# Queries of all tiles projected ahead of the attention loop, together with keys and values

## The reference, cut to what matters

```python
x = x + _L0_cond_ref(x, ...)   # paged attention
x = x + _L1_cond_ref(x, ...)   # 64x64 mix of the tokens, one of 8 weights per batch
x = x + _L2_cond_ref(x, ...)   # x @ W_base.T + low-rank adapter, 1 of 4 per batch
x = x + _L3_cond_ref(x, ...)   # x @ W.T + low-rank adapter, 1 of 8 per batch
```

```python
q = _rope(_rms(q, q_norm_scale), pos)     # rms over the 64 of a head
k = _rope(_rms(k, k_norm_scale), pos)
k_blocks = k_blocks.at[blk, :, off, :].set(k.transpose(0, 2, 1, 3))
v_blocks = v_blocks.at[blk, :, off, :].set(v.transpose(0, 2, 1, 3))
```

## Time and profile before

| what | us |
|---|---|
| median of three runs | 433.83 (431.53 to 435.05) |
| the profiled execution | 432.4 |
| its span, first to last instruction | 430.3 |
| TensorE busy | 414.3 |
| VectorE, ScalarE, GpSimd busy | 308.1, 225.3, 263.7 |

### The profile page before, as it was taken

The page is one execution under the profiler, slowest core; times in us unless marked ns, Lnnn a source line. Parts: engine busy times, 40 slices in busy tenths (PEclk is TensorE's granted clock), DMA queues, the critical chain, the costliest instruction groups (busy, mean ns, idle before and its releaser), DMA issues.

```text
span 430.3 us, 9867 instructions
## 1 busy us (share of the span) xinstructions
PE 414.3 (96%) x2890; PEld 306.0 (71%) x2890; DVE 308.1 (72%) x901; ACT 225.3 (52%) x590; POOL 263.7 (61%) x242
## 2 busy tenths in 40 slices
PE   5999999999899999999999999999999999999987
PEld 1434456846477788887887888778888788788776
DVE  3989797568497777777777767777777777776642
ACT  1232211367356575655756565657566575656641
POOL 3388536655878776767667686767676766734000
PEclk9999999999999999999999999999999999999999
DMA  7187767893655646465564646645565655533211
GB/s 219 44 283 258 259 207 225 249 344 99 199 134 139 195 126 187 121 163 162 137 187 134 189 124 188 145 141 158 145 162 136 171 150 133 145 110 97 56 52 50
DMA packets 76267, 69.08 MB, mean 161 GB/s; under 512 B 50517, under 2 KB 52693, under 8 KB 76215
## 3 DMA queue, kind: packets, MB, share of 16 engines
q1 hardware_dynamic: 57248, 42.03, 33.6%
q0 software_dynamic: 15456, 22.08, 19.3%
q10 hardware_dynamic: 3510, 4.35, 2.8%
HBM read 78.39 MB, written 11.93 MB: 210 GB/s over the span
## 4 chain that ended last, share of the span: by engine, by line
PE 74%; DVE 9%; issue 5%; DMA 4%; POOL 4%; ACT 3%; ACTq 0%; DVEq 0%; POOLq 0%; SPq 0%
PE banks L1131 30%; PE banks L1284 10%; PE banks L1264 9%; PE banks L1144 8%; PE banks L1121 6%; PE banks L1299 4%; POOL windows L529 3%; PE banks L1322 3%; DVE x L902 2%; DMA windows<-kvrows_dram,idx_all 2%; ACT x L677 2%; PE banks L1312 2%; DMA kvb<-kvl_dram 1%; PE banks L1125 1%; DVE prob L989 1%
## 5 line engine op out<-in xcount | busy, mean ns | idle before, releaser
L529 POOL DMA_INDIRECT windows<-newkv,idx_all x78 | 79.3, 1017 | 29.5 <-issue 21.6
L529 POOL DMA_INDIRECT windows<-kvrows_dram,idx_all x78 | 78.6, 1007 | 25.2 <-issue 24.6
L649 ACT ACTIVATE pt_s<-banks 112x384 f32<-112x384 f32 x128 | 56.2, 500 | 64.4 <-PE banks L1121 64.4
L643 ACT ACTIVATE prob<-prob,negmax 128x336 f32<-128x336 f32 x128 | 72.1, 564 | 24.4 <-DVE negmax L989 24.4
L499 POOL TENSOR_TENSOR rstd<-ms,half 128x8 f32<-128x8 f32 x24 | 45.5, 1896 | 54.4 <-DVE ms L922 34.1
L989 DVE CUSTOM_DVE_ANT_0 prob<-banks,mask 128x336 f32<-128x336 f32 x128 | 57.5, 504 | 11.8 <-PE banks L1264 11.4
L1144 PE MATMUL banks<-wkv_s,xt_s 128*128 128x512 f32 x128 | 59.0, 617 | 5.6 <-DMA xt_s<-xt_dram 5.6
L1144 PEld LDWEIGHTS banks<-wkv_s,xt_s 128*128 128x128 f32 x128 | 24.4, 195 | 37.4 <-issue 26.8
L999 DVE TENSOR_SCALAR prob<-prob,rinv 128x336 f32<-128x336 f32 x128 | 45.9, 401 | 2.3
L1264 PE MATMUL banks<-kt_s,qt_s 64*128 64x336 f32 x256 | 44.8, 468 | 0.0
L1131 PE MATMUL banks<-wf_hi,x 128*128 128x512 f32 x120 | 41.7, 408 | 3.0 <-DVE x L902 1.9
(11 more groups left out here) (213 smaller groups left out, 827.6 us busy)
## 6 DMA issues: line engine op xcount, KB each, us to landing
usel<-utab SPq DMA_DIRECT2D x64, 128.0 KB
xt_s<-xt_dram SPq DMA_DIRECT2D x31, 256.0 KB, 4.6
newkv<-kvo SPq DMA_DIRECT2D x16, 256.0 KB, 3.6
stage<-xtok_dram SPq DMA_DIRECT2D x16, 256.0 KB, 13.0
tsel<-ttab SPq DMA_DIRECT2D x64, 64.0 KB
out_dram<-xo ACTq DMA_DIRECT2D x15, 256.0 KB, 6.0
windows<-kvrows_dram,idx_all POOLq DMA_INDIRECT x78
windows<-newkv,idx_all POOLq DMA_INDIRECT x78
```

What stands on the lines that cost most here:

```text
L529: P.indirect_dma_start(kv_s[i][:, c, :], None, newkv if new else kvrows, bass.IndirectOffsetOnAxis(ap=idx_all[:, new * CH + c, b:b + 1], a ...
L643: A.activation(pr, pr, ACT.Exp, bias=negmax[:, g:g + 1], scale=-1.0, accum_out=psum_p[b % 2][:, g:g + 1]).then_inc(S["exp_done"], 1)
L649: A.activation(pt_s[g][:], tb[g % 2][0:KP, 0:CH * 128].rearrange("p (c q) -> p c q", c=CH), ACT.Copy).then_inc(S["pt_ev"], 1)
```

## The change

- The tokens are loaded once. In the front stage ACT rounds each tile (`x_high`), DVE takes the rest (`x_low`), into two alternating buffers `x_s`. From tile 3 on keys and values use these split words with split `wkv` weights, twelve matmuls per tile; tiles 0 to 2 remain plain fp32.
- Each tile's queries follow its keys (tiles 0 to 2 in a row after three key tiles). ACT copies them to `qraw` (128 x 16 x 512 in SBUF) and squares them, DVE sums (`query_sums`) and takes the mean for two tiles, POOL makes the roots of two tiles in one 128x16 power (`root_queries`).
- In the loop `queries`, the reload and split of the tokens, the square, the sums and the root are gone. `query_first` and `query_last` (the rotation) are now in odd k, two tiles ahead, between the mask copy and `ranks` on DVE, and read `qraw`.
- The key banks are two pairs in turn instead of three; queries use banks 4 and 5. Weights of queries and of keys share the places of `wo_s` and `wf_s`. POOL gathers old rows of windows 1 to 3 ahead of the new rows, with the last roots between.

The core of the diff:

```diff
+            x_high(0)
+            for c in range(C):
+                act.wait_ge(l_wkv[c], 16)
+                A.activation(wkv_s[0][:, c], wkv_raw[:, c], ACT.Copy).then_inc(S["wkv_hi"], 1)
...
+            x_high(2)
+            query_ev(0)
+            act.wait_ge(S["tab_ready"], 1)
+            A.activation(nsinx, rest, ACT.Sin, scale=-1.0)
...
+            x_high(3)
...
+            for i in range(2, PAIRS):
+                x_high(2 * i + 1)
+                query_ev(2 * i - 1)
...
+                if 2 * i + 2 < TILES:
+                    x_high(2 * i + 2)
+                query_ev(2 * i)
+                key_pair(i)
...
+            def root_queries(i):
+                pool.wait_ge(S["q_ms"], i + 1)
+                two = [x[:, 2 * i:2 * i + 2, :].rearrange("p t h -> p (t h)") for x in (q_rstd, q_ss)]
+                P.tensor_tensor(two[0], two[1], half[:], ALU.pow).then_inc(S["q_rstd"], 1)
...
+            key_pair(0)
+            query_means(0)
+            for i in range(1, PAIRS):
+                if 2 * i + 3 < TILES:
+                    x_low(2 * i + 3)
+                query_sums(2 * i)
+                if i == 7:
+                    query_first(0)
+                    query_last(0)
+                key_pair(i)
+                if 2 * i + 4 < TILES:
+                    x_low(2 * i + 4)
+                query_sums(2 * i + 1)
+                query_means(i)
+                if i == 1:
+                    index_first()
...
+                if i == 4:
+                    index_rows()
...
             low(t3tab[:, :, :, 0].rearrange("p e c r -> p c e r"), t3tab[:, :, :, 1].rearrange("p e c r -> p c e r"),
                 ob[:].rearrange("p (c e r) -> p c e r", c=C, e=NE3), "t3_hi", 1, "t3_ev")
-            xq_low(1)
+            query_first(1)
+            query_last(1)
...
-                    if t + 2 < TILES:
-                        xq_low(t + 2)
                     if n < NB:
                         mask_at(n)
+                    if t + 2 < TILES:
+                        query_first(t + 2)
+                        query_last(t + 2)
                     if t >= 1:
                         ranks(t - 1)
...
+            def key_tile(n):
+                pe.wait_ge(S["x_lo"], n + 1)
+                if n == PLAIN:
+                    pe.wait_ge(S["wkv_lo"], C)
+                dense3(key_banks(n), lambda p, c: x_s[n % 2][p][:, c, :], lambda p, c: wkv_s[p][:, c, :]).then_inc(S["ka_mm"], 1)
...
+            for n in range(PLAIN):
+                key_tile_plain(n)
+            for t in range(PLAIN):
+                queries(t)
+            for n in range(PLAIN, TILES):
                 key_tile(n)
+                queries(n)
+                if n == 3:
+                    index_blocks()
+                if n == 7:
+                    index_lose()
+                if n == 9:
+                    index_win()
...
                 if k % 2 == 0:
-                    if t + 1 < TILES:
-                        queries(t + 1)
                     keys_t(n)
```

More of the change, by code:

```diff
@@ L163, in build @@
         wcode = sb("wcode", [NB, NW * BLOCK], f16)
-        wt_tok = sb("wt_tok", [NB, NW * BLOCK])
-        wt_ge = sb("wt_ge", [NB, NW * BLOCK])
         idx_all = sb("idx_all", [KP, 2 * CH, NB], i32)
[L167 to L174, removed]
+        half = sb("half", [128, 16])
+        t1, t2 = sb("t1", [128, 8, 64]), sb("t2", [128, 8, 64])
+        wt_tok, wt_ge = (t[0:NB].rearrange("p h d -> p (h d)")[:, 0:NW * BLOCK] for t in (t1, t2))
+        kvi = t1[:].rearrange("p h d -> p (h d)")[:, 512 - NB:512].bitcast(i32)
+        ss, ms, rstd = sb("ss", [128, 8]), sb("ms", [128, 8]), sb("rstd", [128, 8])
+        q_ss, q_rstd = sb("q_sums", [128, TILES, 8]), sb("q_roots", [128, TILES, 8])
         [qrot_w] = words([("qrot_w", [128, 512])])
@@ L259, in build @@
         l_wkv = [sem(f"l_wkv{i}") for i in range(C)]
+        l_wq = [sem(f"l_wq{i}") for i in range(C)]
         l_stage = [sem(f"l_stage{i}") for i in range(STAGES)]
@@ L269, in build @@
         block = ctx.enter_context(nc.Block())
-        splits = [(w[0][:, c], w[1][:, c], src[:, c]) for w, src in ((wq_s, wq), (wo_s, wo)) for c in range(C)]
+        splits = [(wo_s[0][:, c], wo_s[1][:, c], wo[:, c]) for c in range(C)]
+        PLAIN = 3
         PAIRS = TILES // 2
@@ L356, in spread_rows @@
                                  rows.rearrange("p k (c s b) -> p k c s b", c=CH, s=SP_)[:, :, :, s, :]).then_inc(S["idx_ready"], 16)
-            load_keys_x(0)
+            load_x(4)
+            load_x(5)
+            load_x(6)
+            load_x(7)
+            store_pair(0)
+            load_x(8)
+            sp.dma_start(b2_s, b2t).then_inc(S["l_low"], 16)
+            sp.dma_start(a2_s, a2t).then_inc(S["l_low"], 16)
+            load_x(9)
+            store_pair(1)
+            load_rows(wpt_s, wpt, "l_wpt")
+            load_x(10)
+            load_x(11)
+            store_pair(2)
+            sp.wait_ge(S["wkv_lo"], C)
+            load_rows(wt_s, wt, "l_wt")
+            load_x(12)
+            load_x(13)
+            store_pair(3)
+            sp.wait_ge(S["wq_lo"], C)
+            load_rows(wbn_s, wbn, "l_wbn")
+            load_x(14)
+            load_x(15)
+            store_pair(4)
+            spread_rows()
+            sp.dma_start(a3_s[:], a3t).then_inc(S["l_low3"], 16)
+            sp.dma_start(b3_s[:], b3t).then_inc(S["l_low3"], 16)
+            sp.wait_ge(S["qtab_ready"], 1)
+            load_rows(w3_s, w3, "l_w3")
+            store_pair(5)
             load_split(0)
@@ L533, in gather @@
                     ).then_inc(kv_in[i], 16)
-            root("k", 7, 0)
             pool.wait_ge(S["idx_ready"], 16 * SP_)
-            root("q", 1, 1)
             gather(0, 0)
-            root("k", 8, 0)
+            root_keys(6)
+            root_queries(5)
             gather(1, 0)
+            root_queries(6)
+            gather(2, 0)
+            root_keys(7)
+            gather(3, 0)
+            root_queries(7)
             pool.wait_ge(S["row0_stored"], 16)
@@ L602, in evac @@
                 A.activation(dst, src, ACT.Copy).then_inc(S[done], 1)
+            x_high(0)
+            for c in range(C):
+                act.wait_ge(l_wkv[c], 16)
+                A.activation(wkv_s[0][:, c], wkv_raw[:, c], ACT.Copy).then_inc(S["wkv_hi"], 1)
+            x_high(1)
+            for c in range(C):
+                act.wait_ge(l_wq[c], 16)
+                A.activation(wq_s[0][:, c], wq_raw[:, c], ACT.Copy).then_inc(S["wq_hi"], 1)
             key_pair(0)
@@ L950, in _, with split_low @@
+            def split_low(k):
+                dve.wait_ge(S["split_lo"], k)
+                low(splits[k][0], splits[k][1], stage[k % STAGES][:], "split_hi", k + 1, "split_lo")
+            split_low(0)
             low(t2tab[:, :, :, 0].rearrange("p e c r -> p c e r"), t2tab[:, :, :, 1].rearrange("p e c r -> p c e r"),
```

389 lines of the change are left out of this document (159 added, 230 removed).

## The result

The changed kernel takes 455.53 us (median of four runs, 450.81 to 456.01), the kernel before 433.25 (431.53 to 435.05) in the same comparison. The ratio is 1.049, with a 95% interval of 1.042 to 1.056: slower. Forecast were 448.7 us and a range of 439 to 457. The profiled execution is the shortest one, 450.81 us, with a span of 449.0.

What follows compares the result with a forecast made beforehand. TensorE, busy 96%, looked like the bound, but a loop tile without queries waits for attention's low part and saves only 1.77 us. Terms 41.4 - 10.5 - 0.8 + 0.7 + 5.0 - 1.0 - 18.5 = +16.3 on 432.4 gave 448.7 us, range 439 to 457.

Steps and rivals of the forecast that it cites:

- Queries moved to the front: Front stage: fifteen query groups of 2.76 us come to stand before the first folding matmul, +41.4 us.
- Keys in three products: Front stage: thirteen key tiles go from plain fp32 at 3.57 us to split words at 2.76, -10.5 us.
- Waits of the front: Front stage: tile 4's wait for tokens goes, -0.8 us; a new wait before key tile 3, +0.7 (bounds 0 and 2).
- The front ends at 101.8: End of front: first folding matmul moves from 71.04 to 101.8 us by the query, key and wait terms.
- Gathers: First window's keys: POOL's queue of roots and gathers delivers late, so TensorE waits about 5.0 us (0.8 with cheap roots).
- Start of the loop: Loop start: first projection comes 1.0 us earlier relative to the keys, -1.0 us (at most -5.5).
- Loop: Main loop: thirteen tiles lose a query group, gaining 1.42 us each, -18.5 us.
- The rotation's delay: Loop, odd half: rotation between mask and ranks' split on VectorE makes the split 0.35 us late per tile (bounds 0 and 0.7).
- TensorE stays the bound: Rival, whole kernel: every matmul spared in the loop counts, -11.3 us, giving 421.1 us; chance 0.07.
- The losses hide: Rival: roots cost as before, rotation fits before the ranks, loop start gains 5.5; +2.4 us, 434.8 us; chance 0.07.
- The front is bound by VectorE: Rival, front: VectorE's work exceeds a pair's 11.0 us, TensorE waits up to 2 us four times; 457 us; chance 0.12.

Runs made afterwards that it cites:

- experiment 7: Changed kernel with key tiles 3 to 15 as one fp32 product of rounded tokens and weights instead of three split-word products: 460.47 us.
- experiment 5: Changed kernel, order untouched, with 35 extra unread matmuls of 128x512 in TensorE's waits at the start of the loop: 449.37 us.
- experiment 1: Changed kernel with the rotation of a tile's queries moved from the odd half to the even half, between mask and first residual: 445.69 us.
- experiment 6: Extra unread matmuls in each even half but the first: four in the changed kernel, 451.23 us; twelve, plus 8 at loop start, in the both edits kernel, 465.44 us.
- both edits: Changed kernel with rotation in the even half and GpSimd's queue reordered: 444.51 us; with 20 extra unread matmuls at loop start, 441.63 us.

## Why the prediction was right, and by how much it missed

The class was right, and so were the waits and prices that it named, with sizes off by up to 2.7 us. That the median lies in the range is in part luck: the upper end, 457, came from a front bound by VectorE, which did not occur, and what filled that room was the clock, which no step had. Its terms, step by step, against the profiled execution:

- **Queries moved to the front, +41.4.** A group takes 2.80 us when it follows another, not 2.76: +42.0.
- **Keys in three products, -10.5.** Mis-sized. The step divided 7.13 us, the duration of a merged row, by two. Such a duration reaches to the end of the last matmul, which overlaps what follows, and this row stands ahead of a small group of another shape, which starts only 7.07 us after it. Ahead of the folding, the kernel before shows less (TensorE's timeline):

```profile
64.18 7.03 PE L1144 MATMUL banks<-wkv_s,xt_s 128*128 128x512 f32 x16
```

From this row's start to 71.04, the next one's, it is 6.86 us, 3.43 a tile, as in experiment 7 (6.23 less 2.80). A split one takes 2.80, and the term is 13 x 0.63 = -8.2. Starts, not durations, were the number to take.
- **Waits of the front, -0.8 and +0.7.** The wait before key tile 3 is 0.39 us. The wait of 0.76 us for tokens went, but TensorE waits 0.73 us for weights near its start instead. On ScalarE the load and the next instruction read as follows:

```profile
23.55 1.28 ACT L614 ACT_TABLE_LOAD   x1
24.84 0.63 ACT L614 ACTIVATE w_s<-w_s 128x512 f32<-128x512 f32 x1
```

  The next one starts 0.01 us after the load. The Trainium skill (ScalarE: Activation LUTs, What ACT_TABLE_LOAD costs) would have had a drain of 1.38 us more; this row, like that of before, does not show it.
- **The front ends at 101.8.** It ended at 105.02, 3.2 late; 2.9 of these are the two terms above.
- **Gathers, +5.0.** The place was right, the size not. GpSimd's queue, and VectorE's key write that waits in it:

```profile
98.58 3.00 POOL L496 TENSOR_TENSOR q_roots<-q_sums,half 128x16 f32<-128x16 f32 x1
...
112.77 1.67 POOL L491 TENSOR_TENSOR rstd<-ms,half 128x8 f32<-128x8 f32 x1
...
118.78 2.94 POOL L496 TENSOR_TENSOR q_roots<-q_sums,half 128x16 f32<-128x16 f32 x1
121.91 1.05 POOL L523 DMA_INDIRECT windows<-newkv,idx_all  x1 [0.18 <-issue]
```

```profile
105.22 0.17 DVE L854 TENSOR_SCALAR ms<-ss 128x8 f32<-128x8 f32 x1
...
114.48 0.69 DVE L868 TENSOR_TENSOR kvo<-t,rstd 128x512 f32<-128x512 f32 x1 [7.09 <-POOL rstd L491]
```

  The power over 128x16 takes 2.94 to 3.30 us, as taken (3.1). The last key root ended at 114.44, where 112 was forecast, the new rows' gather started at 121.91 (119.5) and landed at 127.95 (126.3 to 127.7). TensorE asked 3.8 us later than forecast, so it waited 2.28 us only. The moment at which the keys' transposes start, 128.00 against 121.9 + 5.0 = 126.9, is off by 1.1: that the two misses met is luck.
- **Start of the loop, -1.0.** From the first keys' transposes to the first projection it is 33.24 us against 125.19 - 91.17 = 34.02 before: -0.8. The wait of 3.18 us behind the rotation of the third tile's queries was foreseen as a delay.
- **Loop, -18.5.** The tile quoted is 1.49 shorter, others less. From the first projection to that of the last tile it is 277.73 us before (125.19 to 402.92, and the earlier trace rows) and 258.91 at full clock (161.32 to 420.23 in experiment 5): -18.8. The rotation's delay, taken at 0.35, is 0.20 to 0.27 by experiment 1.
- **What was missing: the clock.** No step asked what TensorE's new waits do to its clock. In the profiled execution this is 1.4 us (its run, 450.81, against experiment 5, 449.37), in the median about 6.

At full clock the changed kernel takes 449.37 us and the forecast was 448.7; the sum of +16.3 stands against +16.7 in that comparison. What the median lies above that goes with the clock.

The rivals: *TensorE stays the bound* fell by experiment 6, where 14 us of matmuls cost nothing. *The losses hide* fell with the roots at 3 us and the rotation's delay. *The front is bound by VectorE* fell for this kernel, which has no wait from 27.82 to 128.00.

What is left at full clock with both edits, 441.63 - 432.21 = 9.4 us, is the price of having the queries ahead of the loop. An estimate from the numbers above: 42.0 for the queries ahead, -8.2 for the keys, and in the loop -1.74 for each of the 14 groups of tiles 2 to 15 (that of tile 1 only hid a wait), -24.4, give +9.4. The trace of that run bears the two parts out: the keys' first transposes come 33.9 us later than before (125.03 against 91.17), and from there to the last tile's projection it is 24.7 less (287.09 against 311.75). No version tried here beats the kernel before.

## What to carry to other kernels

Work on the busiest engine is worth only what its neighbours leave uncovered: before you move it, look for a place in the trace where the loop already runs once without it, and price it there. Take costs of repeated groups from the distance of their starts, not from the duration of a merged row. Where a change opens waits on TensorE, ask what they do to the granted clock; a few matmuls that nobody reads show it in one run.

## What the runs showed of the hardware that was not expected

Waits can cost more than they last. In the changed kernel the clock is granted at 0.50 for about 7 us from 157.6 to 164.4 us, among waits that left TensorE busy for 1.57 of 5 us, and the twelve matmuls of the first projection take 4.51 us in the chain instead of 3.06. One execution has a mean clock of 0.992 and one such fall, the others 0.984 or 0.985, by which they have about two; the times spread from 450.81 to 456.01 us, and kept busy they lie within 0.3 us. The Trainium skill (TensorE: Matmul & The Clock Gate, HAM oscillation — how this bites in real kernels) tells of a kernel whose clock drops while its matmuls wait for DMAs; here the waits are mostly for VectorE, and the rows agree.
